# An attention and low-rank expert kernel on one core: GpSimd divides the probabilities before its products for the rotary embedding instead of after them, in two of eight steps

## The reference

```python
q, k, v = (layernorm(x) @ W for W in (Wq, Wk, Wv))       # 16 heads of 64
q, k = rotary(q), rotary(k)                              # q * cos + swap_pairs(q) * sin
logits = where(causal, q @ k.T, -1e9) / 8
out = softmax(logits) @ v @ Wo
x = x + layernorm(out)
f = layernorm(x)
scores = 8 * softmax(f @ Wr.T + br)                      # 8 experts
low = f @ A.T                                            # rank 16 for each expert
x = x + layernorm(2 * sum_h scores[h] * (low[h] @ B[h].T))
```

## Time and profile before

| | |
|---|---|
| median of 3 runs | 1244.17 us (1242.47 to 1245.31) |
| profiled execution, its own time | 1249.05 us |
| its span | 1247.3 us |
| busy share of the span: PE, DVE, ACT, POOL | 89%, 66%, 54%, 41% |
| PE's granted clock, mean over the span | 0.966 |
| slots / turns behind them | to about 975 us / 272 us |
| instructions of POOL | 476 |

### The profile page before, as it was taken

The page is one execution under the profiler, slowest core; times in us unless marked ns, Lnnn a source line. Parts: engine busy times, 40 slices in busy tenths (PEclk is TensorE's granted clock), DMA queues, the critical chain, the costliest instruction groups (busy, mean ns, idle before and its releaser), DMA issues.

```text
span 1247.3 us, 20995 instructions
## 1 busy us (share of the span) xinstructions
PE 1104.8 (89%) x5616; PEld 904.3 (73%) x5616; DVE 827.3 (66%) x2200; ACT 667.8 (54%) x1499; POOL 513.7 (41%) x476
## 2 busy tenths in 40 slices
PE   3899999999998875899998999999977899999994
PEld 2678777777777654678777777877766688888873
DVE  8566676667677666666767767667675566666663
ACT  5455555555555554555555556555555345555442
POOL 2154544546454323244635445445444133322321
PEclk9999999999999988999999999999998899999995
DMA  5010102111011212011101111010123322222210
GB/s 219 35 39 27 59 8 63 42 29 59 8 59 29 93 43 92 19 43 31 59 8 61 31 38 46 25 59 13 62 74 97 124 97 91 91 93 101 101 51 34
DMA packets 37500, 73.45 MB, mean 59 GB/s; under 512 B 3152, under 2 KB 19536, under 8 KB 37456
## 3 DMA queue, kind: packets, MB, share of 16 engines
q1 hardware_dynamic: 37456, 72.92, 17.9%
HBM read 56.14 MB, written 16.78 MB: 58 GB/s over the span
## 4 chain that ended last, share of the span: by engine, by line
PE 33%; issue 23%; DVE 20%; ACT 14%; POOL 6%; DVEq 1%; ACTq 1%; DMA 1%; POOLq 0%; SPq 0%
PE bank L1039 21%; PE bank L1079 8%; DVE prob L839 4%; ACT pT_hi L592 4%; DVE rot_c L871 3%; ACT o_low L635 3%; POOL swapped L483 2%; POOL rot_c L481 2%; DVE k_hh L883 2%; ACT prob L581 2%; ACT q_hl L611 2%; DVE swapped L866 1%; DVE pT_lo L857 1%; PE bank L1106 1%; DVE q_hl L876 1%
## 5 line engine op out<-in xcount | busy, mean ns | idle before, releaser
L1079 PE MATMUL bank<-big_hi,w_hi 128*128 128x512 f32 x768 | 335.0, 436 | 16.1 <-DVE big_lo L828 16.1
L581 ACT ACTIVATE prob<-prob,nmax 128x128 f32<-128x128 f32 (+3 forms) x256 | 144.1, 563 | 366.6 <-DVE nmax L839 365.2
L471 POOL TENSOR_SCALAR prob<-prob,rinv 128x128 f32<-128x128 f32 (+3 forms) x256 | 146.6, 573 | 398.7 <-DVE rinv L849 398.5
L1079 PE MATMUL bank<-big_hi,w_lo 128*128 128x512 f32 x768 | 306.6, 399 | 0.0
L1079 PE MATMUL bank<-big_lo,w_hi 128*128 128x512 f32 x768 | 304.9, 397 | 0.0
L857 DVE TENSOR_TENSOR pT_lo<-bank,pT_hi 128x128 fp32r<-128x128 f32 (+3 forms) x256 | 123.9, 484 | 125.6 <-ACT pT_hi L592 125.2
L1079 PEld LDWEIGHTS bank<-big_hi,w_hi 128*128 128x128 f32 x768 | 147.9, 193 | 32.3 <-issue 17.7
L1079 PEld LDWEIGHTS bank<-big_hi,w_lo 128*128 128x128 f32 x768 | 146.3, 191 | 34.1
L1079 PEld LDWEIGHTS bank<-big_lo,w_hi 128*128 128x128 f32 x768 | 148.0, 193 | 11.5
L1106 PE MATMUL bank<-ident,prob 128*128 128x128 f32 x640 | 116.4, 281 | 35.9 <-POOL prob L471 30.2
L1106 PEld LDWEIGHTS bank<-ident,prob 128*128 128x128 f32 x640 | 82.0, 143 | 82.3 <-POOL prob L471 31.2
(11 more groups left out here) (104 smaller groups left out, 2092.0 us busy)
## 6 DMA issues: line engine op xcount, KB each, us to landing
w_raw<-in_wqkv SPq DMA_DIRECT2D x48, 512.0 KB, 3.3
attention_out<-o_sum SPq DMA_DIRECT2D x64, 128.0 KB, 2.3
xin<-attention_out SPq DMA_DIRECT2D x16, 512.0 KB, 4.7
xres<-in_x SPq DMA_DIRECT2D x16, 512.0 KB, 3.4
out<-res SPq DMA_DIRECT2D x16, 512.0 KB, 2.6
xin<-in_x SPq DMA_DIRECT2D x14, 512.0 KB, 3.7
w_raw<-in_wo SPq DMA_DIRECT2D x6, 512.0 KB, 4.8
prob<-in_x SPq DMA_DIRECT2D x2, 512.0 KB, 6.6
```

What stands on the lines that cost most here:

```text
L471: pool.tensor_scalar(p, p, rinv[:, q % 4:q % 4 + 1], 1.0, ALU.mult, ALU.mult).then_inc(prob_done, 1)
L581: act.activation(prob[:, q % 4, 0:n], prob[:, q % 4, 0:n], ACT.Exp, scale=-1.0, bias=nmax[:, q % 4:q % 4 + 1], accum_out=rsum[:, q % 4:q % ...
L1079: done = pe.matmul(grp_ps[(b + k) % 2][:, :], w, xt, start=at == 0, stop=at == GROUP_MM - 1)
```

## The change

In `slot` on POOL the call of `divide` moves ahead of the call of `rotate`:

```diff
                 for s in range(STEPS):
+                    divide(u, s)
                     if real(u) and s in (3, 6):
                         rotate(u, s // 6)
-                    divide(u, s)
                     if s == 1 and b == 0 and real(u) and late(n, 1):
                         w_low(2, n)
```

## The result

| | before | with the change |
|---|---|---|
| median | 1244.14 us (1242.47 to 1245.31, 4 runs) | 1358.71 us (1357.46 to 1359.55, 4 runs) |
| ratio to before | | 1.0921, 95% interval 1.0902 to 1.094 |
| profiled execution: time, span | 1249.05, 1247.3 us | 1358.11, 1356.3 us |
| PE's mean granted clock | 0.966 | 0.928 |
| the 16 turns behind the slots | 272 us | 272 us |

The change costs 114.6 us; the forecast was 110, 1354 us. In the traces all of it is in the slots: the first transpose of the turns starts at 1089.0 us instead of 979.8.

The account below looks back on a forecast made before the run. A ring of DVE, ACT and POOL sets the pace and PE follows; 8.3 us a pair over 13 pairs, 108, plus 8 irregular, 116, at 0.95 gives 110: 1244 + 110 = 1354 us, range 1310 to 1385.

Parts of the forecast that it names:

- two slots that differ only in DVE's stalls: Consecutive slots of 27.80 and 25.27 us with the same PE projections and scores, read as showing what a DVE delay costs.
- The two places: DVE's rotation sum after POOL's products of step 3 (+1.67 or +2.2 us) and of step 6 (+2.2 us a slot).
- the sign that was named: DVE's wait at L871 for POOL's products grows from 6.1 us to some 9 us a pair, 120 us or more.
- The term that was mis-sized: Second slot's step 3: without POOL's divide beside it, DVE's sum takes 0.69 instead of 1.07 us, leaving +1.67 us.
- The discount: A microsecond of DVE delay costs about 0.95 us of slot, which turns 116 us into 110 us.
- The irregular slots: Slots 1, 17 and 14 to 16, outside the 13 regular pairs, have cover; estimated at 8 us for the five.
- the cover of the normalisation: In slots 14 to 16 the next batches' normalisation is worked in; in slot 16 it hides 1.4 of 2.2 us.
- PE's gain: PE's wait for step 6's divide, some 1.3 us a slot, is shortened; costed at 0 because PE follows.
- the clock rival: PE's longer waits for the copy of k lower its clock, 1 us a slot unhidden: 1385 us, 7 in 100.
- The shared port: In the first slot's step 7, w_low starts ahead of k_low and delays it too: 0.2 us a pair, outside the sum.

Follow-up runs that it names:

- each run alone: Two runs against the kernel before: POOL divides before its products only in step 3, 1294.06 us, or only in step 6, 1308.38 us.

## Why the prediction was right

**What bounds.** The prediction read the pace from two slots that differ only in DVE's stalls, and took PE for a follower though it is the busiest engine. The runs with less work for PE show this directly: 576 products less, ratio 1.0004.

**The two places.** Each was costed by itself, and each run alone gave it: in the pair shown 3.97 and 4.37 us against 3.87 and 4.4, together 8.28 against 8.3. By the average of all regular pairs it is 3.61, 4.11 and 7.79, so the regular pairs cost 13 x 7.79 = 101 us and not 108. DVE's wait for the products, the sign that was named at some 9 us a pair and 120 in all, is 8.2 and 114.6 us.

**The term that was mis-sized.** The forecast took the stretch of DVE's sum beside POOL's divide, which the change takes away, from one pair: 1.07 against 0.69 us, once. In the trace before, 36 of the 52 sums of the regular slots were stretched, those of step 7 too:

```profile
373.97 0.94 DVE L871 TENSOR_TENSOR rot_c<-rot_c,swapped 128x512 f32<-128x512 f32 x1
```

Together they took 11.3 us more than 0.69 us each, and with the change all 52 take 0.69. The forecast had counted 13 x 0.38 = 4.9 us of that. The other 6.3 are 0.49 us a pair, which is what lies between 8.27 and 7.79.

**The discount.** As a price of delay the factor 0.95 doesn't hold. It came from 2.53 us of slot against 2.7 us of stall, and the stall left out a wait of DVE for ACT:

```profile
276.25 0.68 DVE L896 TENSOR_TENSOR o_sum<-bank,o_low 64x512 f32<-64x512 f32 x1 [1.28 <-ACT o_low L635]
...
304.18 0.68 DVE L896 TENSOR_TENSOR o_sum<-bank,o_low 64x512 f32<-64x512 f32 x1 [1.41 <-ACT o_low L635]
```

That is 0.13 us more in the later slot. With it the stalls differ by 3.18 - 0.38 - 0.14 - 0.13 = 2.53 us, as the slots do: a delay of DVE cost what it lasted. The factor made up, by luck, for the term that was mis-sized (0.95 x 8.3 = 7.9).

**The irregular slots.** Slots 14 to 17 took 10 us more in the traces (160.65 against 150.67), where 8 were estimated for them and slot 1. In slots 14 and 15 DVE waits for the products 0.76 us in all, as the cover of the normalisation made one expect. Before slot 2 and behind slot 32 the traces differ by 2 us the other way, and 101 + 10 - 2 = 109 us is the difference of the two spans: 1358.11 us for the profiled execution, forecast 1359. The medians lie 114.6 apart because the profiled execution of the kernel before was 4.9 us above its median and that of the changed kernel 0.6 below. So no trace shows the last 5.5 us of the 114.6.

**PE's gain.** It was costed at nothing, and it came to nothing: 23 us less of one wait, 69 us more of another.

**The clock.** PE's waits of 4 us did bring its granted clock down, as the rival said, to 0.92 in a regular pair:

```profile
329.32 0.47 PE L1039 MATMUL bank<-k_hh,q_hl 128*128 128x128 f32 x1 [4.21 <-DVE k_hh L883]
```

From 329 to 334 us it was granted 0.50, which is 1.2 GHz. In this slot DVE's negate waits 0.78 us for PE's scores, but DVE's sum behind it waits for POOL until 343.81 in any case, 1.56 us more. What was lost is 0.2 us earlier in the slot: the reciprocal of step 3 ended 11.26 us after the slot's start, where it had been 11.06. In the changed kernel with less work for PE it is 11.06 again, and a regular pair is 0.19 us shorter on average (61.02). So what the clock rival named cost some 2 us in all at most (1.4 by the medians) and not 31; PE's spare time covered the rest. And the long wait came once a pair, not in each slot: the other was 1.77 us at 358.67.

**The shared port.** The order of w_low and k_low did turn round in step 7: k_low took 2.66 us and the copy 0.42, where before they took 0.68 and 2.51. The rule of the Trainium skill (SBUF — State Buffer, on the shared port pair) foretold this, down to the side that is held up. The price worked out from it was 0.2 us more a pair, and that loss didn't come: from the start of the sum in step 7 to the next slot it is 4.88 us (324.33 to 329.21) where it was 4.98 (293.54 to 298.52), 0.1 us less.

## What to carry to other kernels

Before an edit moves an instruction ahead of another on one engine, ask what each of them waits for: the one that could run in the other's waiting time has to stand first. A busy share of 93% doesn't make an engine the bound; two stretches with the same work and different stalls, or a run with less work for that engine, tell whether it leads or follows. What a period costs is read from all its repetitions: here the one shown was off by half a microsecond in eight. And where waits of three engines grow together, the largest total needn't be the cause: switch the suspected places on one at a time.

## What the runs showed of the hardware that was not expected

- Which of DVE and POOL held the other up was decided by a start 0.2 us sooner. Moving ACT's pT_hi by one place let q_low in 0.24 us ahead of w_low, and it took 0.81 instead of 1.77 us. With POOL's wait behind k_low, another 13 us went.
- With PE at work on fewer products the granted clock in the pair fell (0.95 against 1.00) while the time stayed. Here the lower clock of a follower was no loss.
